# A twelve-layer decoder on one core: its two mixtures of experts get a tile per expert loaded without indices, overflow tiles whose gathers are skipped where empty, and outputs scattered by token

## The reference, cut to what matters

```
logits = x @ gate_w.T                          # 64 experts
topv, topi = jax.lax.top_k(logits, TOP_K)      # 8 of them
rw = softmax(topv)
gate, up = x @ gu_w[e].T                       # 128 + 128 wide
out = sum over e of W[:, e] * (silu(gate) * up) @ dp_w[e].T
out = out + sigmoid(x @ sh_gate1_w.T) * shared_expert(x)
```

## Time and profile before

| | |
|---|---|
| median of 3 runs | 3539.7 us (3533.76, 3539.7, 3539.82) |
| the profiled execution's own time | 3534.41 us |
| its span | 3532.6 us |
| mean granted clock of TensorE | 0.914 |
| PE, DVE, ACT, POOL busy | 85%, 44%, 29%, 13% of the span |
| mixture 5, first router matmul to last batch | about 1425 to 1749 us |
| mixture 11, first router matmul to last batch | about 2882 to 3511 us |

### The profile page before, as it was taken

The page is one execution under the profiler, slowest core; times in us unless marked ns, Lnnn a source line. Parts: engine busy times, 40 slices in busy tenths (PEclk is TensorE's granted clock), DMA queues, the critical chain, the costliest instruction groups (busy, mean ns, idle before and its releaser), DMA issues.

```text
span 3532.6 us, 36213 instructions
## 1 busy us (share of the span) xinstructions
PE 3000.9 (85%) x14276; PEld 1880.4 (53%) x14276; DVE 1560.5 (44%) x2609; ACT 1036.7 (29%) x2982; POOL 469.2 (13%) x494
## 2 busy tenths in 40 slices
PE   7889989998889999789598989999787877999951
PEld 4445454554655565467354555555444455777740
DVE  5510277103835555410365656566365667000026
ACT  3210161101723333212172223223135441444420
POOL 0000000000000000022201212120010001555555
PEclk9889989999899999899798999999798867999985
DMA  3011102100011110179300010011000002999964
GB/s 149 17 44 42 60 15 70 43 29 1 17 36 45 43 47 30 48 283 326 95 24 11 31 45 32 19 39 36 24 18 22 1 1 77 368 361 366 364 216 116
DMA packets 78377, 319.04 MB, mean 90 GB/s; under 512 B 13408, under 2 KB 13408, under 8 KB 66432
## 3 DMA queue, kind: packets, MB, share of 16 engines
q0 software_dynamic: 39264, 186.30, 15.0%
q1 hardware_dynamic: 16880, 90.19, 7.2%
q10 hardware_dynamic: 22064, 40.25, 3.1%
HBM read 274.80 MB, written 41.88 MB: 90 GB/s over the span
## 4 chain that ended last, share of the span: by engine, by line
PE 71%; DVE 17%; ACT 7%; issue 3%; POOL 2%; DMA 1%; POOLq 0%; ACTq 0%; SPq 0%; DVEq 0%
PE P L878 32%; PE P L880 14%; PE P L1199 9%; PE P L1097 3%; PE P L1079 3%; ACT A L1314 3%; PE P L886 3%; DVE A L1475 2%; PE P L891 2%; DVE A L1916 1%; POOL A L2000 1%; DVE A L1727 1%; DVE A L1725 1%; DVE A L1726 1%; ACT A L1431 1%
## 5 line engine op out<-in xcount | busy, mean ns | idle before, releaser
L878 PE MATMUL P<-A,W 128*128 128x400 f32 (+1 forms) x1888 | 691.4, 506 | 10.3 <-DVE A L1755 6.8
L1246 ACT ACTIVATE A<-P 128x400 f32<-128x400 f32 (+5 forms) x770 | 411.8, 543 | 969.1 <-PE P L880 452.3
L878 PEld LDWEIGHTS P<-A,W 128*128 128x128 f32 x1888 | 362.5, 195 | 283.9 <-issue 33.7
L2000 POOL DMA_INDIRECT A<-experts,A x141 | 134.3, 952 | 2010.2 <-DVE A L1901 1855.3
L886 PE MATMUL P<-C,A 128*128 128x128 f32 (+4 forms) x1553 | 230.4, 273 | 163.1 <-DVE A L1925 130.6
L878 PE MATMUL P<-X,W 128*128 128x400 f32 x864 | 336.6, 528 | 34.4 <-DVE X L1579 30.1
L1199 PEld LDWEIGHTS P<-A 128*128 128x128 f32 x2704 | 328.6, 194 | 69.2 <-issue 41.0
L1199 PE MATMUL P<-A 128*128 128x128 f32 x2704 | 329.6, 277 | 1.4 <-ACT A L1246 1.4
L886 PEld LDWEIGHTS P<-C,A 128*128 128x128 f32 (+4 forms) x1553 | 181.8, 149 | 206.1 <-DVE A L1925 140.1
L1916 DVE TENSOR_TENSOR A<-P,A 128x128 f32<-128x128 f32 (+1 forms) x141 | 44.9, 318 | 552.9 <-ACT A L1431 552.9
L878 PEld LDWEIGHTS P<-X,W 128*128 128x128 f32 x864 | 170.1, 201 | 165.6 <-DVE X L1579 34.1
(11 more groups left out here) (230 smaller groups left out, 3746.1 us busy)
## 6 DMA issues: line engine op xcount, KB each, us to landing
W<-weights SPq DMA_DIRECT2D x60, 1024.0 KB, 4.8
slot_outputs<-A ACTq DMA_DIRECT2D x141, 256.0 KB
W<-weights SPq DMA_DIRECT2D x32, 448.0 KB, 3.4
x_by_token<-A ACTq DMA_DIRECT2D x16, 200.0 KB
A<-experts,A POOLq DMA_INDIRECT x141
A<-x_by_token,A POOLq DMA_INDIRECT x141
W<-weights SPq DMA_DIRECT2D x8, 256.0 KB, 2.6
C<-constants SPq DMA_DIRECT2D x1, 1990.5 KB, 17.2
```

Source lines behind the costliest of these rows:

```text
L878: self.e.matmul(out, a, b, start=i == 0, stop=False)
L1246: self.e.activation(out, in_, ACT.Copy).then_inc(*self.of(*item))
L2000: self.e.indirect_dma_start(out, None, table, bass.IndirectOffsetOnAxis(ap=idx, axis=0)).then_inc(sem, 16)
```

## The change

Both mixtures keep their number of tiles, but divide them otherwise. Each expert has a tile of its own (16 and 64 tiles), for its first 128 pairs; its weights are known without any list, so SP loads them with plain transfers, from a new class `SyncE` that takes over SP's queue. The other tiles (NO = 12 and 49, "further tiles") take what goes beyond 128; POOL gathers their weights, and an index beyond the table is skipped, so an empty tile moves nothing. They stand between the own tiles in a fixed sequence `c.seq`. In place of the token, the list holds the row `token * kk + choice`, from which both the token (a shift) and the output row follow. Each tile's y is scattered by POOL (`give`) to row `token * kk + choice` of `token_outputs`; ACT stores nothing there. At the end SP reads each batch's rows as one plain transfer of 100 rows (1.6 MB in mixture 11), and DVE adds `direct` of the kk choices (2 of 2, 5 of 8) with their gates; in mixture 11 PE adds the last 3 by matmuls with diagonal matrices of the gates.

The step `lists` is cut into `ranks`, `places`, `by_token`, `listed`, `indices`, which stand between the parts of the shared expert, and the rest of `choose` becomes `weigh_choice`, behind the lists. The gates of each choice (`gate_of`) and their diagonals (`gate_diagonals`) are made inside the tile loop, one per step from step 8. There are two free steps between `fetch` and `xturn` in both mixtures now (mixture 5 had none).

```diff
     def moe_sub(self, n, pre, E, kk, nf, table):
-        c.NT = (T * kk + 127 * E) // 128
+        c.NO = (T * kk - kk) // 128
+        c.NT = E + c.NO
...
+            c.R = 3
+            c.places = lambda: [(self.ar(12096, 3072), stored), (self.ar(21280, 3072), [("proj", "sdown", n, NB - 1)]),
+                                (self.ar(0, 3072), [("choice", n, "gates")])]
...
+            c.direct = 5
+            c.YJ = [self.ar(12096 + 4096 * i, 8, 512) for i in range(3)]
+            c.R = 8
...
+        for e in range(E):
+            c.seq.append((c.NO + e, e))
+            while o < c.NO and e < E - kk and (o + 1) * (E - kk - R) <= (e + 1 - R) * c.NO:
+                c.seq.append((o, None))
+                o += 1
...
     def moe(self, c, tail):
-        for f in range(c.nf):
-            for h in range(2):
-                yield "shared", c, f, h
+        shared = [("shared", c, f, h) for f in range(c.nf) for h in range(2)]
+        yield "ranks", c
+        yield from shared[:1]
+        yield "places", c
+        yield from shared[1:2]
+        yield "by_token", c
+        yield from shared[2:]
+        yield "listed", c
+        yield "indices", c
+        yield "weigh_choice", c
         for b in range(NB):
             yield "shared_down", c, b
-        yield "lists", c
-        idle = 2 if c.nf == 1 else 0
-        stages = ["fetch"] + [None] * idle + ["xturn", "up", "down"]
+        stages = ["fetch", None, None, "xturn", "up", "down", "give"]
+        gates = [("gate_of", c, j) for j in range(c.kk)]
+        if c.direct < c.kk:
+            gates += [("gate_diagonals", c, b) for b in range(NB)]
         for t in range(c.NT + len(stages) - 1):
             for i in range(len(stages) - 1, -1, -1):
                 if stages[i] and 0 <= t - i < c.NT:
                     yield stages[i], c, t - i
+            if t >= 8 and gates:
+                yield gates.pop(0)
...
     def combine(self, c, b):      # TensorE
+        self.wait_ge(self.at("acc", c.n, b, c.direct - 1))
...
+        for k in range(4):
+            f = slice(128 * k, 128 * k + 128)
+            for j in range(c.direct, c.kk):
+                self.e.matmul(ps[:, k, :], y[0:S, j, f], c.DG[0:S, b, j - c.direct, :], start=j == c.direct, stop=False)
+            i = self.e.matmul(ps[:, k, :], c.ACC[0:S, b, f], self.c["ident"][0:S, 0:S], start=False, stop=True)
...
     def fetch(self, c, i):        # GpSimdE
-        if i >= len(c.WT):
-            self.wait_ge(self.at("proj", "edown", n, i - len(c.WT)))
-        self.gather(c.WT[i % len(c.WT)], c.table, c.WI[:, i:i + 1], "got_w", n, i)
+        if expert is None:
+            self.wait_ge(self.at("proj", "edown", n, i - c.R))
+            self.rows(c.places()[i % c.R][0], None, c.table, c.WI[:, d:d + 1], 128 * c.E - 1, "got_w", n, i)
...
+    def give(self, c, i):
+        d = c.seq[i][0]
+        self.wait_ge(self.at("y", c.n, i))
+        self.rows(c.YD[:, :], c.YI[:, d:d + 1], c.Y[:, i % 4, :], None, T * c.kk - 1, "given", c.n, i)
...
+    def experts(self, c):         # SyncE
+        for i, (d, expert) in enumerate(c.seq):
+            if expert is None:
+                continue
+            place, needs = c.places()[i % R]
+            for item in needs if i < R else [("proj", "edown", c.n, i - R)]:
+                self.wait_ge(self.at(*item))
+            self.dma(f"expert{i % R}", place, c.table[128 * expert:128 * expert + 128, :], "got_w", c.n, i)
+        for i in range(c.NT):
+            self.wait_ge(self.at("given", c.n, i))
...
+            self.dma(f"given{b}", y[0:S], c.YD[S * c.kk * b:S * c.kk * (b + 1), :].rearrange("(t j) n -> t j n", j=c.kk), "got_y", c.n, b)
```

More of the change, by code:

```diff
@@ new lines, in moe_sub, with before @@
+        R = c.R
+        c.seq, o = [], 0
+        for e in range(E):
[3 more added lines that the diff above has]
+                o += 1
+        assert o == c.NO and all(e is not None for _, e in c.seq[:R]) and all(e is not None for _, e in c.seq[-kk:])
+        return c
+    def before(self, *name):
+        p = self.load(*name).index
+        return range(p - RING + 1, p)
@@ L785, in moe @@
                     yield stages[i], c, t - i
-        first = [("norm_add", c, 0), ("norm_centre", c, 0), ("norm_scale", c, 0)]
+            if t >= 8 and gates:
+                yield gates.pop(0)
+        first, tail = ([s for s in steps if s] for steps in self.norms(c))
         for b in range(NB):
-            for j in range(c.kk):
-                yield "collect", c, b, j
+            yield "collect", c, b
             yield "combine", c, b
@@ L853, in steps @@
                 "latent": self.latent, "back": self.back, "router": self.router, "x_out": self.x_out, "shared": self.shared,
-                "shared_down": self.shared_down, "lists": self.lists, "xturn": self.xturn, "up": self.up, "down": self.down,
+                "shared_down": self.shared_down, "ranks": self.ranks, "places": self.places, "by_token": self.by_token,
+                "listed": self.listed, "indices": self.indices, "xturn": self.xturn, "up": self.up, "down": self.down,
                 "combine": self.combine, "gates": self.gates}
@@ L1155, in shared_down, with ranks @@
             q.free = p.free
-    def lists(self, c):
-        E, NT = c.E, c.NT
+    def ranks(self, c):
         for g in range(2):
@@ L1161, in lists, with places, by_token @@
             self.wait_ge(self.at("chosen", c.n))
-            self.turns([(P[0:E, ss(b)], c.MK[0:S, 4 * g + b, :]) for b in range(4)], S, "turn", "mask", c.n, g)
+            self.turns([(P[0:c.E, ss(b)], c.MK[0:S, 4 * g + b, :]) for b in range(4)], S, "turn", "mask", c.n, g)
+    def places(self, c):
         P = self.take(("plan", "tri", c.n), ("end", c.n))
         self.wait_ge(self.at("tiles_of", c.n))
-        self.e.matmul(P[0:E, 0:1], self.c["tri"][0:E, 0:E], self.k.small[0:E, 8:9], start=True, stop=True).then_inc(*self.of("plan", "tri", c.n))
-        per = min(512 // E, NB)
+        self.e.matmul(P[0:c.E, 0:1], self.c["tri"][0:c.E, 0:c.E], self.k.small[0:c.E, 8:9], start=True,
+                      stop=True).then_inc(*self.of("plan", "tri", c.n))
+    def by_token(self, c):
+        per = min(512 // c.E, NB)
         for g in range(0, NB, per):
@@ L1853, in lists, with places @@
+    def places(self, c):
+        E, n, sm = c.E, c.n, self.k.small
+        mark, after = self.marks(c)
+        more, own, far, end = (sm[0:E, i:i + 1] for i in (8, 9, 11, 10))
+        self.e.tensor_scalar(own, self.c["lane"][0:E, :], 128.0, 128.0 * c.NO, ALU.mult, ALU.add).then_inc(*mark("own"))
+        after("own")
         self.wait_ge(self.at("plan", "tri", n))
         P = self.ps("plan", "tri", n)
-        self.e.tensor_scalar(base, P[0:E, 0:1], 128.0, None, ALU.mult).then_inc(*mark("base"))
@@ L1856, in lists @@
-        self.e.tensor_tensor(end, P[0:E, 0:1], tl, ALU.add).then_inc(*self.of("end", n))
+        self.e.tensor_scalar(far, P[0:E, 0:1], 128.0, -128.0, ALU.mult, ALU.add).then_inc(*mark("far"))
+        self.e.tensor_tensor(end, P[0:E, 0:1], more, ALU.add).then_inc(*self.of("end", n))
+        after("far")
+        self.e.tensor_tensor(far, far, own, ALU.subtract).then_inc(*mark("step"))
+        after("step")
+        self.e.tensor_scalar(c.FILL[0:E, :], c.RK[0:E, :], 128.0, far, ALU.is_gt, ALU.mult).then_inc(*mark("beyond"))
@@ L1860, in lists, with by_token @@
-        self.e.tensor_scalar(c.CM[0:E, 0:NT], self.c["tiles"][0:E, 0:NT], end, None, ALU.is_ge).then_inc(*self.of("ended", n))
+        self.e.tensor_scalar(c.CM[0:E, 0:c.NO], self.c["tiles"][0:E, 0:c.NO], end, None, ALU.is_ge).then_inc(*self.of("ended", n))
+    def by_token(self, c):
+        E, n, kk = c.E, c.n, c.kk
+        mark, after = self.marks(c)
         per = min(512 // E, NB)
+        some = lambda a: a[0:S, :, 0:kk]
+        self.e.scalar_tensor_tensor(out=some(c.DV), in0=bc(self.c["token"][0:S, :], [S, NB, kk], 2), scalar=float(kk),
+                                    in1=bc(self.c["slots"][0:S, 1:kk + 1], [S, NB, kk]), op0=ALU.mult, op1=ALU.add).then_inc(*mark("rows"))
@@ L1991, in big, with rows @@
             self.e.tensor_tensor(qc, qc, qs, ALU.add).then_inc(*self.of("roped", c.n, h, half, j))
-    def gather(self, out, table, idx, *item):
+    def rows(self, out, at_out, in_, at_in, bound, *item):
         n, self.gathers = self.gathers, self.gathers + 1
```

286 lines of the change are left out of this document (171 added, 115 removed).

## The result

The changed kernel takes 3564.03 us (median of 4 runs, 3562.62 to 3566.3), the kernel before 3536.73 (4 runs) beside it: ratio 1.008, interval 1.0063 to 1.0098. The prediction said 3508 and faster. The profiled execution has 3563.1 us where the one before had 3532.6, so 30.5 more.

A forecast was written before the change was run, and what follows sets the result against it. Both loops were taken as TensorE's, mixture 11's end as a chain of gathers. Own time 3534.4 -25.0 -2.4 +5.1 -6.3 -0.5 gave 3505.3, set to 3508 for the median; range 3495 to 3521, with rivals 3488 to 3530.

The forecast's parts named there:

- Front of mixture 11, -25.0: Before mixture 11's loop: lists beside the shared expert bring the first `down` to 2973.0 from 2998.03, gain 25.0 us.
- Loop of mixture 11, -2.4: Mixture 11's tile loop: stays TensorE's at 3.60 us a tile; part of the 3.3 us lost at its start returns.
- It fits, with 14% to spare ... I take 0: Mixture 11's loop: POOL's five indirect transfers take 6.2 us of each 7.2 us pair of tiles, so they cost 0.
- The third rival: Mixture 11's loop: POOL becomes the bound from 1.44 us a transfer; 3546 at 1.6, 3582 at 1.75; chance 0.11.
- at 1.6 it is +38: Mixture 11's loop: if each POOL transfer took 1.6 us with its gap, 38 us more, 3546 us in all.
- every gather compares its indices: POOL in mixture 11's loop: each transfer now checks its indices against a bound, an argument for a price above 1.25 us.
- End of mixture 11, +5.1: After mixture 11's loop: first addition 6.7 us later, batches at 10.4 us gain 1.6; net cost 5.1 us.
- Mixture 5, -6.8: Mixture 5: first `down` 6.3 us earlier, with lists beside the shared expert, and 0.5 gained at its end.
- the first: End of mixture 11: full clock or bound by reads, 8.2 us a batch, 17.6 less, 3490 us; chance 0.15.
- The second (queues): Front and end of mixture 11: late lists, low clock and reads at 133 GB/s cancel the gain, 3532 to 3537; chance 0.09.

The follow-up runs named there:

- e5: The changed kernel, unedited, run again beside the kernel before: 3521.38 us, ratio 0.9963, loop of mixture 11 403.5 us.
- e14: Changed kernel with the further tiles' weights loaded plainly by SP (other experts), GpSimd only gathering x and scattering y: 3525.03 us, ratio 0.9976.
- e13: Changed kernel with y in mixture 11 stored plainly by ScalarE, no scatter (sums of wrong rows): 3522.82 us, ratio 0.9965.
- e1: Changed kernel with 8 buffers for y instead of 4 in mixture 11: 3518.62 us, ratio 0.9956.
- e7: Changed kernel with VectorE's additions of the next batch ahead of the addition of x, in both mixtures: 3478.57 us, ratio 0.9852.
- e4: Changed kernel with VectorE adding all 8 rows of a token in mixture 11, no diagonals on TensorE: 3491.08 us, ratio 0.9879.
- e11: Changed kernel with VectorE's additions one batch ahead and each read issued as 96 partitions and 4: 3514.60 us, ratio 0.9946.
- e8: The changed kernel, unedited, run once more in another group: 3561.10 us, ratio 1.0081, loop of mixture 11 436.4 us.
- e15: Changed kernel with GpSimd also issuing skipped gathers for own tiles' weights from mixture 11's ninth tile, SP loading none: 3674.22 us, one run.
- e12: Changed kernel with 8 buffers for y in mixture 11, repeated in a later group: 3565.16 us, ratio 1.0085.
- e9: Changed kernel with each 100-row read at a mixture's end issued as 96 partitions and 4: 3559.50 us, ratio 1.0074.

## Why the prediction was wrong, by its steps

**Front of mixture 11, -25.0: right.** Measured -24.7 (first `down` 25.39 earlier, 0.71 of it from mixture 5). VectorE's first one-hot starts at 2930.45, forecast 2929.8; TensorE's product of it is the row at 2931.04. The sum of evacuations and small steps behind it held too.

**Loop of mixture 11, -2.4: the step that failed.** Measured +37.5 in the first record, -3.6 in e5. The failed step is "It fits, with 14% to spare ... I take 0": I took GpSimd's own 0.95 + 0.30 us as all that a transfer costs. On GpSimd that was nearly right, 1.02 to 1.04 and 0.30. What the runs showed in its place is a cost outside GpSimd: on a stalling chip five transfers for two tiles make `up` tell its end late, and the loop gets through one transfer in 1.59 us on average; with four it takes 406.5 us and with three 403.5 (e14, e13). The third rival named this place and the threshold of 1.44 us, and its "at 1.6 it is +38", counted from a loop that gained 2.4, is within 2 us of the measured +37.5. Its mechanism was another, though: GpSimd itself taking 1.6 us, with x late at TensorE. GpSimd takes 1.33 and x is not late, so a good part of that hit is luck. It got 0.11 as "every gather compares its indices" was the only reason I had for a higher price. What I overlooked: in the trace of before these transfers never came five for two tiles, since GpSimd waited there for TensorE (every 1.79 us one). The one place where they came nearly back to back was the end, 62 in 97 us, one every 1.56, GpSimd busy 71.71 of them. I named that row for the rival and set it aside with VectorE as the reason. Its spacing as an upper bound would have made the loop's margin negative. It is no measurement of the same limit: the instructions are longer there (1.16), and 8.2 of the 97 us are waits for VectorE's additions.

On the chips of e1 to e7 the same step was right, and with it the direction: e5 has 3521.38 us, ratio 0.9963, inside the range of 3488 to 3530. That doesn't rescue the forecast: a margin of 14% that is worked out from the busy time on one engine, in one trace, is a risk, and 0.11 was too little for it.

**End of mixture 11, +5.1: mis-sized, measured +18.5 on either kind of chip** (e5: 16.3 to the first addition and 105.9 from there). Two terms. The first read took 13.1 us from its issue (3422.38 to 3435.52), where I had 8.2 and 1.6 of latency. The 1.6 was a slip: 6.8 less 4.5 is 2.3. The rest is the rate: in these 13.1 us the reads move 164 GB/s and not 200, some 2.15 MB by that rate, of which the first read is 1.64; three are in flight together, and the others have the rest. And a batch takes 11.63 us instead of 10.4: 32 passes at the low clock are 7.14 us, 0.22 each, not 0.183, so these products with diagonals took longer than the three transposes that I took the number from (why, no run says); the five additions were 3.9 instead of 4.2. Times eight that is 9.8 of the 10.1 us by which the batches miss. e4 confirms it: with the passes back at 4 a batch, the end is 29.3 us shorter, though VectorE adds three rows more. Moving three additions to TensorE was a loss of 3.7 us a batch: that TensorE is idle in the end says nothing on what its work costs when VectorE waits for it.

**Mixture 5, -6.8: measured -0.7**, first `down` 4.5 earlier (forecast 6.3), then 4.2 us lost to the same stall in its loop, 179.35 against 175.17, a term that the sum did not have. On the chip of e1 to e4 the last addition of x stands at 1743.6 to 1744.4, 4.6 to 5.4 earlier.

**The other rivals.** The clock at the end was 0.50 throughout, so the first fell. The second (queues) took the reads at 133 GB/s; they ran at 164 before the first addition and at 179 from 3440 to 3460 us, and lengthened the first wait alone.

## What to carry over

When a change gives an issuing engine more transfers, its busy time per transfer is not the whole price: other engines can pay, and only over a long stretch. Take the mean spacing of the densest long stretch that the trace has as the safe price, and if the plan needs a denser one, give that risk a real chance. GpSimd's 1.33 us in a short row says nothing of what a hundred tiles will pay. Run the unedited kernel in every group of experiments: a stall that goes with the chip makes every edit look like its cure, as e1 to e4 did. And of the two kernels here neither is best: e7, the changed kernel with the additions one batch ahead, is 1.48% faster than before where nothing stalls (0.9837 to 0.9867), and e11, the same with its reads split, still 0.54% (0.993 to 0.9963) where it does.

## What the runs showed of the hardware that was not expected

- Groups of runs on different chips differ for one and the same program: 3521.4 us (e5) and 3561.1 us (e8), while the kernel before took 3534.3 and 3533.0 beside them. Mixture 5's loop tells the two kinds apart: 179.0 to 179.3 us in the first record and in e8 to e15, 175.2 in e1 to e7.
- On the stalling kind, many of GpSimd's indirect transfers close together make matmuls of TensorE tell their end late: 2.4 us at the end of a row of eight that are 1.33 us apart (mixture 5), 1.1 to 1.3 us about every fourth tile at 5 transfers for two tiles (first record and e12; in e8 to e11 less regularly), mostly 3 to 4 us at 6 (e15). GpSimd's own 1.01 to 1.05 us a transfer don't change, and on the other kind 17 in a row at 1.33 us had no such effect (e5).
- The mean over 280 us on the stalling kind is one transfer every 1.59 us (the first record) and 1.66 us (e15).
- A bounded gather keeps GpSimd busy for 1.03 to 1.04 us and a scatter for 1.02, against 0.95 without bounds.
- Reads of 1.6 MB from rows by token, three in flight, move 179 GB/s on ten engines (e8, 3421.4 to 3441.4 us) and 205 on sixteen (e9, 3420 to 3440 us).
